# Probabilities of a cross-attention kernel stored with the context chunk as the innermost axis

## What is computed

```python
q = jnp.einsum('bte,ef->btf', emb, Wq) + bq
k = jnp.einsum('bml,le->bme', latent, Wk) + bk
v = jnp.einsum('bml,le->bme', latent, Wv) + bv
w = jnp.einsum('bte,bme->btm', q, k) * scale
w = jax.nn.softmax(w, axis=1)
pred = jnp.einsum('btm,bme->bte', w, v)
x = pred + emb
# layer norm over the last axis, times gamma, plus beta
```

## Time and profile before

| | us |
|---|---|
| median of 3 runs (lowest, highest) | 142.45 (141.98, 142.91) |
| the profiled execution, its own time | 142.72 |
| its span in the trace | 141.0 |

### The profile page before, as it was taken

How to read it: one execution, slowest core, us unless ns; L and a number is a source line. 1 busy time by engine, 2 the same in 40 slices (tenths; PEclk the granted TensorE clock), 3 DMA queues, 4 the chain that set the end, 5 groups by cost and what they waited for, 6 DMA issues and landing times.

```text
span 141.0 us, 2976 instructions
## 1 busy us (share of the span) xinstructions
PE 134.5 (95%) x1046; PEld 130.2 (92%) x1046; DVE 115.1 (82%) x224; ACT 79.6 (56%) x283; POOL 60.8 (43%) x61
## 2 busy tenths in 40 slices
PE   6999999999999999999999999999999999999940
PEld 6899999999998999999999999999999999999940
DVE  0689995996996779999999976878789976797983
ACT  4267098677276925467474829474747546386420
POOL 1000000027304580733849370629475643629791
PEclk9999999999999999999999999999999999999998
DMA  4899999965087495995988799696996965535314
GB/s 152 294 411 417 424 307 394 333 227 204 13 251 274 184 364 153 380 346 188 342 294 297 291 308 382 225 324 211 328 335 227 383 251 203 212 103 196 144 73 150
DMA packets 10814, 37.33 MB, mean 265 GB/s; under 512 B 1200, under 2 KB 1456, under 8 KB 10800
## 3 DMA queue, kind: packets, MB, share of 16 engines
q1 hardware_dynamic: 9424, 34.79, 69.6%
q10 hardware_dynamic: 1376, 2.36, 4.4%
HBM read 33.87 MB, written 3.28 MB: 263 GB/s over the span
## 4 chain that ended last, share of the span: by engine, by line
PE 89%; POOL 5%; issue 2%; ACT 1%; DVE 0%; POOLq 0%; DVEq 0%
PE ps_S L423 29%; PE ps_U L437 26%; PE ps_Y L458 10%; PE ps_U L396 6%; PE ps_Y L396 6%; POOL xT_in L978 3%; PE ps_Y L340 2%; POOL xT_in L966 2%; PE ps_S L344 1%; PE ps_w L446 1%; PE ps_U L503 1%; PE ps_U L350 1%; PE ps_c L411 1%; PE ps_U L355 1%; ACT xT_in L600 1%
## 5 line engine op out<-in xcount | busy, mean ns | idle before, releaser
L582 ACT ACTIVATE expo<-scores,negmax 121x100 f32<-121x100 f32 x96 | 35.0, 365 | 30.9 <-DVE negmax L753 30.9
L423 PE MATMUL ps_S<-G,ctxT_in 128*121 128x100 f32 (+1 forms) x384 | 43.4, 269 | 0.0
L423 PEld LDWEIGHTS ps_S<-G,ctxT_in 128*121 128x121 f32 (+1 forms) x384 | 42.1, 185 | 0.0
L437 PEld LDWEIGHTS ps_U<-prob,ctx_in 121*128 121x128 f32 x336 | 39.4, 192 | 0.9
L437 PE MATMUL ps_U<-prob,ctx_in 121*128 121x100 f32 x336 | 39.6, 274 | 0.0
L955 POOL TENSOR_TENSOR prob<-expo,rinv 121x600 f32<-121x600 f32 x16 | 19.2, 1202 | 30.6 <-DVE rinv L760 30.4
L966 POOL TENSOR_TENSOR xT_in<-x_in,xT_in 128x512 f32<-128x512 f32 (+1 forms) x13 | 17.1, 1315 | 19.8 <-issue 8.9
L749 DVE TENSOR_TENSOR scores<-ps_S,c_rows 121x600 f32<-121x600 f32 x16 | 12.5, 782 | 10.3 <-PE ps_S L423 7.4
L764 DVE TENSOR_REDUCE probsum<-prob 121x100 f32<-121x600 f32 x16 | 19.8, 1237 | 1.0 <-POOL prob L955 0.7
L582 ACT ACTIVATION_READ_ACCUMULATOR expo<-scores,negmax 121x1 f32 x96 | 17.9, 187 | 0.0
L971 POOL TENSOR_TENSOR rstd<-vareps,neg_half 128x1 f32<-128x1 f32 (+1 forms) x13 | 7.1, 549 | 23.3 <-DVE vareps L791 23.1
(11 more groups left out here) (120 smaller groups left out, 185.7 us busy)
## 6 DMA issues: line engine op xcount, KB each, us to landing
ctx_in<-ctx SPq DMA_DIRECT2D x16, 768.0 KB, 4.9
ctxT_in<-ctxT SPq DMA_DIRECT2D x16, 722.0 KB, 5.1
xT_in<-xT SPq DMA_DIRECT2D x8, 400.0 KB, 8.5
x_in<-x SPq DMA_DIRECT2D x12, 256.0 KB, 4.6
out<-xT_in ACTq DMA_DIRECT2D x8, 256.0 KB, 4.0
wqk<-Wqk SPq DMA_DIRECT2D x4, 388.0 KB, 4.6
out<-xT_in SPq DMA_DIRECT2D x3, 256.0 KB, 2.0
wv_in<-Wv SPq DMA_DIRECT2D x1, 512.0 KB, 15.7
```

Source lines behind the costliest of these rows:

```text
L423: last = nc.tensor.matmul(ps_scores(c)[0:rows(c), :], ctxT_in[:, q, l * M + c * MP:l * M + c * MP + rows(c)], G[:, l, bass.ds(b * T, T)], ...
L437: last = nc.tensor.matmul(ps_U[:, q, l * T:(l + 1) * T], ctx_in[0:rows(c), q, c, l * P:(l + 1) * P], prob[0:rows(c), q, c * T:(c + 1) * T] ...
L582: last = nc.scalar.activation(expo[0:MP, q, c * T:(c + 1) * T], scores[0:MP, q, c * T:(c + 1) * T], ACT.Exp, bias=negmax[0:MP, q, c:c + 1] ...
```

## The change

`expo` and `prob` keep their size, but the element of chunk c and token t now lies at t * 6 + c. So `exponentials` writes 100 elements with a step of six, `probabilities` walks 600 neighbouring elements with the six reciprocals repeated for each token, `chunk_sum` reads 600 neighbouring elements, and the matmuls of lines 437 and 503 read 100 moving elements that are six elements (24 bytes) apart. The order of instructions, their numbers, shapes and waits on each engine stay the same. (The lines of the kernel after are up to three higher.)

```diff
+        def token_major(ap):
+            return ap.rearrange("p (t c) -> p t c", c=MC)
...
                         last = nc.tensor.matmul(ps_U[:, q, l * T:(l + 1) * T],
                                                 ctx_in[0:rows(c), q, c, l * P:(l + 1) * P],
-                                                prob[0:rows(c), q, c * T:(c + 1) * T], start=(c == 0), stop=(c == MC - 1))
+                                                token_major(prob[0:rows(c), q, :])[:, :, c], start=(c == 0), stop=(c == MC - 1))
...
                     last = nc.tensor.matmul(ps_U[:, l, l * T:(l + 1) * T],
                                             ctx_in[0:rows(c), b % 2, c, l * P:(l + 1) * P],
-                                            prob[0:rows(c), b % 2, c * T:(c + 1) * T], start=(c == 0), stop=(c == MC - 1))
+                                            token_major(prob[0:rows(c), b % 2, :])[:, :, c], start=(c == 0), stop=(c == MC - 1))
...
-                    last = nc.scalar.activation(expo[0:MP, q, c * T:(c + 1) * T], scores[0:MP, q, c * T:(c + 1) * T],
+                    last = nc.scalar.activation(token_major(expo[0:MP, q, :])[:, :, c], scores[0:MP, q, c * T:(c + 1) * T],
...
-                nc.vector.tensor_reduce(probsum[0:MP, batch_tokens(b)], prob[0:MP, q, :].rearrange("p (c t) -> p t c", t=T),
+                nc.vector.tensor_reduce(probsum[0:MP, batch_tokens(b)], token_major(prob[0:MP, q, :]),
                                         AX.X, ALU.add).then_inc(probsum_set, 1)
...
-                nc.gpsimd.tensor_tensor(prob[0:MP, q, :].rearrange("p (c t) -> p c t", t=T),
-                                        expo[0:MP, q, :].rearrange("p (c t) -> p c t", t=T),
-                                        rinv[0:MP, q, :].unsqueeze(2).to_broadcast([MP, MC, T]),
+                nc.gpsimd.tensor_tensor(token_major(prob[0:MP, q, :]), token_major(expo[0:MP, q, :]),
+                                        rinv[0:MP, q, :].unsqueeze(1).to_broadcast([MP, T, MC]),
                                         ALU.mult).then_inc(prob_set, 1)
```

## The result

The kernel after takes 168.78 us (median of 4 runs, 168.59 to 169.05) against 142.28 us for the kernel before in the same comparison: ratio 1.185, interval 1.182 to 1.188. It is 26.5 us slower. The forecast was 169.6 us with a sum of 27.1 us.

A forecast was written before the change was run, and what follows sets the result against it. PE was taken as the bound, U passes held by weight loads; 384 x 70.7 ns = 27.1 us on the 142.45 us median gave 169.6 us, other engines nothing. Own range 161.2 to 176.5 us, whole range 141.8 to 178 us.

The forecast's parts named there:

- What bounds the kernel: PE until about 126 us; each U pass held by its weight load, 111.3 ns, the moving stream hidden under it.
- a low share of PEld: In the profile after, the busy share of PE's weight loads should fall well under 92%.
- The price of a column: U matmuls, lines 437 and 503: 1.82 ns per stepped column, a pass 70.7 ns longer, 384 passes 27.1 us.
- Rival 1: 384 U passes: a stepped column takes 1.11 ns or less, streaming stays under the weight load, 142.3 us; chance 0.20.
- Rival 2: U passes: only DVE's surcharge of 0.77 ns is added, 1.23 ns a column, 4.5 us, 147 us; chance 0.09.
- Rival 3: U passes: each element is fetched twice, 3.64 ns a column, 239 us; partial forms over 177 us; chance 0.11.
- the 2.50 ns for a step of 24 words: DVE figure from the skill, applied to U's stepped read: an estimated 53 us more, time 196 us.
- Rival 4: ACT's stepped exponential writes become late, needing 0.23 us more each before DVE's reciprocal slips; 144 us or so; chance 0.02.
- POOL: The product slows at worst from 1202 to 1545 ns, 0.34 us per batch, hidden by 3.9 us of cover: nothing.
- DVE: chunk_sum falls from 1237 to about 778 ns, 7.3 us less busy time, costed at nothing.
- The tail: 48 of the 384 U passes are late_U, 36 after 126.9 us; final adds wait for PE, so these count too.

The follow-up runs named there:

- columns80: The kernel after, but each U matmul streams only the first 80 of the 100 tokens: 154.71 us, ratio 1.083.
- split_step4: The kernel before, but 32 fp32r passes of the projection read their moving operand with a step of four elements: 147.86 us, ratio 1.040.
- all_but_pe: The kernel after, but the U matmuls read 100 neighbouring elements again: 142.72 us, ratio 1.001.
- write_alone: The kernel before, but ACT writes expo and POOL reads it with a step of six, prob staying chunk by chunk: 145.11 us, ratio 1.018.

## Why the prediction was right, step by step

- **What bounds the kernel.** Right. The rule that a pass takes the longer of weight load and stream was used for the sum, and `columns80` confirmed it (144.2 ns, expected 143.7). The sign that I gave for it, a low share of PEld, was wrong: 93%.
- **The price of a column.** The number was right, 1.82 ns forecast, 1.80 measured, and so the sum, 27.1 us against 26.5. The reason was only half right, and that the number came out was in part luck. I had read 16 bytes per 1.82 to 1.86 ns out of the fp32r passes as a limit of the memory and put it beside DVE's 1.82 ns for a lone element. `split_step4` takes a new 16 bytes every 0.90 ns, so there is no such limit. That four fp32r neighbours took the same 1.82 ns as DVE's lone element was a coincidence. What stands is that a float32 column on a line of its own costs 1.80 ns, twice a neighbouring one. Had the stepped operand been fp32r, the same argument would have forecast twice its real price.
- **Rival 1** (the stream stays under the weight load) is false at six elements and true at two. Its threshold of 1.11 ns fits: 0.92 ns beside neighbours hides, 1.35 ns at a step of three does not.
- **Rival 2** (surcharge of 0.77 ns) is false: 3 us per 24 passes were expected for it, 4.31 came.
- **Rival 3** (two fetches for each column) may hold as a mechanism but with half the price for a fetch, 0.90 ns, so its 239 us did not come. Beside it I weighed the 2.50 ns for a step of 24 words that the "Vector Engine (DVE) Microarchitecture Reference" of the Trainium skill (section "Measured stream behaviour on trn2") gives for DVE. No such rise shows on PE: 1.79 ns at 4, 1.80 at 6, 1.83 at 100 elements; a step of 24 itself was not run.
- **Rival 4** (ACT late) is false: the pace of the exponentials did not change at all, less than the 0.1 us each that I had allowed. The record, 462 ns, is a little over the 365 to 450 that I named.
- **POOL.** 1404 ns lies within the 1202 to 1545 that I gave, and `all_but_pe` shows it hidden. But the way I counted its cover, 3.9 us until PE needs `prob`, is not enough: `write_alone` lost 2.6 us with a product only 0.4 us longer. Some of DVE's instructions can be held up by POOL's, and the values wait for DVE, so that path needs a cover of its own.
- **DVE.** 774 ns as forecast (778), and worth nothing, as `all_but_pe` shows. DVE's busy time fell by 9.4 us instead of 7.3; most of what `chunk_sum` doesn't explain is `rinv`, 170 ns for 299 on average (2.1 us), which in the kernel after hardly ever meets lines 966 and 978 on POOL.
- **The tail.** All 48 passes counted, as forecast: the difference of the U pieces (26.2 us) leaves only 0.3 us for everything else.

The page "SBUF — State Buffer" of the Trainium skill (section "Specifications (TRN2)") asks for at least two hits in each 16-byte line for full bandwidth. For float32 matmuls the runs agree at two elements of step (two hits, no loss; below the weight load a smaller price could not be seen) and from four on (one hit, twice the time). For fp32r with three elements the loss is nearly full (0.885 ns against 0.90) though one line in three is hit twice; the measurement decides.

## What to carry to other kernels

Ask first what holds a matmul pass: here the weight load, 0.87 ns for each stationary column, gave a moving column 1.11 ns of room. A layout that makes a matmul operand step by 16 bytes or more doubled its read (moving float32, steps of 4, 6 and 100 elements: 1.80 for 0.92 ns a column; fp32r 0.90 for 0.456 and stationary 1.77 for 0.87, both run at a step of 4), so the step belongs on an engine with idle time, as it was on DVE before, where `chunk_sum` paid 0.46 us per batch for nothing lost. Don't price an engine's access by the pace of another one: use a row of the same engine and the same type, or measure one.

## What was not expected of the hardware

- The clock: with stepped stationary reads the granted clock fell to 0.50 (1.2 GHz) in stretches, with PE busy all the time, and cost about 29 us on top of the 44.5 us of the passes.
- fp32r and float32 differ at a step of three: 1.94 times the neighbouring pace against 1.47 times.
- `rinv` on DVE, both inputs in SBUF, ends only behind line 966 or 978 on POOL where it finds one running: 0.17 us alone, up to 1.11 us so (`write_alone`). `U_lo`, with an input in PSUM, is not held.
- A stepped write costs ACT no pace: 365 and 462 ns are lengths of the record, the starts stay 0.36 us apart.
